# Sorted token rows widened from 130 to 144 words, and new rank numbers for the planner

## The reference, cut to what matters

```
x = x + 0.5 * ffn0(ln(x))      # gated low-rank mixture: softmax gate, 8 experts of rank 16
x = x + mamba(ln(x))           # in-projection, width-4 convolution, scan over 2048 steps, out-projection
x = x + 0.5 * ffn0(ln(x))
x = x + 0.5 * moe(ln(x))       # 8 experts, top 2 of each token, and a shared expert
x = x + attn(ln(x))            # linear attention, 16 heads of 8
x = x + 0.5 * moe(ln(x))
```

## Time and profile before

| | us |
|---|---|
| median of 3 runs | 842.06 (841.09 to 842.87) |
| the profiled execution | 838.86, of which the span is 837.5 |
| TensorE busy | 766.9 (92% of the span) |
| of it fillers (L558) | 70.6 |
| VectorE, ScalarE, GpSimd busy | 573.4, 559.3, 516.7 |
| mean granted TensorE clock | 0.975 |

### The profile page before, as it was taken

How to read it: one execution, slowest core, us unless ns; L and a number is a source line. 1 busy time by engine, 2 the same in 40 slices (tenths; PEclk the granted TensorE clock), 3 DMA queues, 4 the chain that set the end, 5 groups by cost and what they waited for, 6 DMA issues and landing times.

```text
span 837.5 us, 15645 instructions
## 1 busy us (share of the span) xinstructions
PE 766.9 (92%) x4762; PEld 604.3 (72%) x4762; DVE 573.4 (68%) x1960; ACT 559.3 (67%) x1305; POOL 516.7 (62%) x650
## 2 busy tenths in 40 slices
PE   7999999998898999988999999999999999997992
PEld 6668668785877776677877758867587876695771
DVE  5387579988899868767648884767975668633112
ACT  4888788796779688676677754685446577533551
POOL 4137527737837763898854487747775565774652
PEclk9998999998999999999999999999999999998997
DMA  9930000001100120212123212311422111217215
GB/s 326 406 140 2 1 1 1 2 2 39 52 1 8 36 61 23 62 42 75 43 71 92 56 52 71 119 30 49 127 65 59 44 49 33 68 57 221 83 58 169
DMA packets 43890, 60.70 MB, mean 72 GB/s; under 512 B 7083, under 2 KB 32939, under 8 KB 43595
## 3 DMA queue, kind: packets, MB, share of 16 engines
q1 hardware_dynamic: 33987, 39.36, 14.9%
q0 software_dynamic: 9536, 19.68, 7.0%
q10 hardware_dynamic: 288, 0.67, 0.2%
HBM read 26.61 MB, written 33.07 MB: 71 GB/s over the span
## 4 chain that ended last, share of the span: by engine, by line
PE 29%; POOL 22%; DVE 19%; issue 14%; DMA 8%; ACT 7%; SPq 0%; POOLq 0%; DVEq 0%; ACTq 0%
POOL sorted_x L1805 10%; PE psum L563 6%; PE psum L834 5%; PE psum L854 5%; POOL sent_y L1815 4%; DMA sent_y<-e_y,e_sx 3%; DVE m_cv L1066 2%; DMA e_sx<-sorted_x 2%; POOL m_ch L1743 1%; PE psum L558 1%; PE psum L643 1%; POOL m_ch L1746 1%; PE psum L876 1%; PE psum L735 1%; DMA c_ys<-sent_y 1%
## 5 line engine op out<-in xcount | busy, mean ns | idle before, releaser
L1815 POOL DMA_INDIRECT sent_y<-e_y,e_sx x170 | 166.9, 982 | 101.0 <-ACT e_y L1643 60.6
L1805 POOL DMA_INDIRECT sorted_x<-g_xn,r_slot x128 | 128.9, 1007 | 38.3 <-issue 28.3
L834 PE MATMUL psum<-gu_w,e_sx 128*128 x340 | 114.4, 466 | 0.7 <-issue 0.3
L1338 DVE TENSOR_TENSOR e_h<-e_h,psum 128x352 f32<-128x352 f32 x88 | 43.5, 505 | 95.8 <-ACT e_h L1635 95.7
L854 PE MATMUL psum<-d_w,e_h 88*128 x680 | 90.6, 280 | 2.6 <-DVE m_ch L1090 1.7
L854 PEld LDWEIGHTS psum<-d_w,e_h 88*128 88x128 f32 x680 | 84.2, 194 | 11.8 <-issue 9.5
L1643 ACT ACTIVATE e_y<-psum,e_sx 128x128 f32<-128x128 f32 x170 | 52.5, 363 | 49.0 <-PE psum L854 46.4
L834 PEld LDWEIGHTS psum<-gu_w,e_sx 128*128 128x128 f32 x340 | 60.1, 192 | 28.7 <-issue 7.1
L558 PE MATMUL psum<-ones 128*128 128x128 f32 x468 | 70.6, 293 | 3.7 <-POOL ones L1839 2.7
L1461 ACT ACTIVATE e_h<-psum 88x512 f32<-88x512 f32 x88 | 49.3, 574 | 36.3 <-PE psum L563 36.1
L558 PEld LDWEIGHTS psum<-ones 128*128 128x128 f32 x468 | 64.0, 207 | 7.2 <-issue 3.0
(11 more groups left out here) (265 smaller groups left out, 1933.9 us busy)
## 6 DMA issues: line engine op xcount, KB each, us to landing
e_sx<-sorted_x SPq DMA_DIRECT2D x82, 130.0 KB, 2.2
sorted_x<-c_ys SPq DMA_DIRECT2D x8, 975.0 KB, 19.7
c_ys<-sent_y SPq DMA_DIRECT2D x14, 512.0 KB, 4.8
sent_y<-e_y,e_sx POOLq DMA_INDIRECT x170, 2.3
sorted_x<-c_ys SPq DMA_DIRECT2D x4, 520.0 KB, 15.9
xs<-in_x SPq DMA_DIRECT2D x8, 256.0 KB, 7.2
sorted_x<-g_xn,r_slot POOLq DMA_INDIRECT x128
out<-xs SPq DMA_DIRECT2D x7, 256.0 KB, 3.7
```

Source lines behind the costliest of these rows:

```text
L834: last = e.matmul(two.banks[j].tile[:, 0:2 * IEXP], e_xT[k % SXS][:, j, :], gu_w[:, bass.ds(which[j] * (2 * IEXP), 2 * IEXP)], start=True, ...
L1805: e.indirect_dma_start(out=sorted_x[CHAIN_OF[g]], out_offset=bass.IndirectOffsetOnAxis(ap=r_slot[n][:, k, t:t + 1], axis=0), in_=rows[:, j ...
L1815: e.indirect_dma_start(out=sent_y[CHAIN_OF[g]], out_offset=bass.IndirectOffsetOnAxis(ap=e_sx[k % SXS][:, j, DM:DM + 1].bitcast(U32), axis= ...
```

## The change

The row of `sorted_x`, `g_xn` and `e_sx` grows from 130 to 144 words (576 bytes, a multiple of 64). EMPTY_ROWS goes from 15 to 14, so that `unused` still fits its tile (2016 words in place of 1950); the number of clearing DMAs stays 14. The 14 new words of each row in `g_xn` are set to zero once, by six memsets on GpSimd at the start. All rank tables have new numbers. The code of the stages is the same; lines from L1846 on move down by two.

```diff
-SENT = DM + 2
-EMPTY_ROWS = 15
+SENT = DM + 16
+EMPTY_ROWS = 14
...
-GATED = [-1497.43, -960.07, 235.63, 1059.97, -7983.26, -1651.28, -41121.12, -217474.65, -604379.49, -849493.79, 2025218.58, 2025219.86, 8147161894221.35, 6245036494796.88, 9945646075954.11, 4444332380753.18]
-SORTED = [-2090.99, 301.91, -1657.3, -35988.35, -539663.99, 494449.79, 1200.61, -2160876050918.97]
-SCATTERS = [-2102.77, -374.8, -3399.65, -875901.89, -1060663.42, -857995.38, 5024367203900.46, 6425558899159.76]
-PAIRED = [3666.91, -3680.96, -321147.12, -1076870.97, 1382196855041.05, 1516605603609.4, -19347204475812.39, -9460026041.51]
-PACE = [-1050.91, 43.59, 25911.68, 66896.07, 3527377721.29, 766276379171.74, 29710191757825.85, 70005041151.74]
-SENDS = [3831.16, -3506.7, -134882.98, -1595699.93, -816918.01, -3539908697451.05, 1830812465821.03, 40706064242.79]
+GATED = [-1612.12, -1346.31, 356.81, 1334.2, -2048.0, -1910.79, -101456.5, -269539.84, -35665391501.77, -410616469058586.44, 442199635419.06, 502734914612.92, 1552142795094442.8, -43274453972354.49, 1981894470395523.5, -1118408670439937.5]
+SORTED = [-2246.32, 1258.21, -3334.22, -36096.98, 1448911033546.08, 505016298414.97, -38562742267150.11, -598217000560311.0]
+SCATTERS = [344.97, -1816.91, -3712.68, -35939813952.68, -208340876042141.6, 29237801575472.65, 2778915344593449.5, 3026567072914857.0]
+PAIRED = [3695.57, -3222.66, -365441.24, -36419792749.16, -13224196291645.03, 4210780943512.94, -454154928134527.56, -1647290385447738.5]
+PACE = [-1122.96, 10.56, 23989.31, 68581921.67, 162723903713.99, 139491480699914.4, 1174660669112806.5, 6393651726682.28]
+SENDS = [3649.32, -3839.35, -55107.17, -36203751788.7, 32539564149069.16, 1265605042228444.5, 2774040927401660.5, 40704983681.34]
...
-KV = [-3161.35, -3477.72, -218282.65, -36067.44, 2173065613425.52, -902319.35, 2271812405962.31, 3814568062581.78]
+KV = [-3032.32, -3409.14, -276152.59, -80207.69, -36066720278.38, 1451984751506.02, -410688839305970.75, 143702267412699.53]
...
             e.memset(r_before[:, 1, 0:E1], 0.0).then_inc(*S.up("const"))
+            for n in range(KEPT):
+                e.memset(g_xn[n][:, :, DM + 2:SENT], 0.0)
```

More of the change, by code:

```diff
@@ L98 @@
 ATANH = [2.0 / (2 * k + 1) for k in range(8)]
[L102 to L105, removed]
+FIRST = [-2922.08, -2401.94, -1709.16, -1700.91, -1583.08, -1612.43, 376.46, 417.78]
@@ L106 @@
+AGAIN = [-960.85, -1032.71, -2157.16, -2516.16, 476.01, -2241.58, -3016.99, -3080.49]
+MAMBA = [-1739.62, -1693.62, -1056.95, -1066.84, -2194.24, 381.12, 3735.88, -5322.46]
+CHUNK_AT = [-1087.79, -1852.23, -1069.29, -1161.19, -1772.88, -855.06, -1041.13, -1030.56, -1025.62, -776.8, -1586.73, -455.61, -903.83, -1622.58, -1583.54, -1591.63, 367.78, 296.26, 347.39, -2403.13, 260.12, 414.62, 440.87, 370.95, -7605.45, -7662.02, -4057.85, -3749.59, -3745.39, -3740.45, -3713.07, -3404.84]
 TAP_STEP = -2.4
@@ L107 @@
 FOLD_AT = 35.0
-FINISH = [-1555.21, -913.54, -856.1, -2166.89, 1061.16, -3355.47, -3891.89, -3376.38]
-GATED = [-1497.43, -960.07, 235.63, 1059.97, -7983.26, -1651.28, -41121.12, -217474.65, -604379.49, -849493.79, 2025218.58, 2025219.86, 8147161894221.35, 6245036494796.88, 9945646075954.11, 4444332380753.18]
-SORTED = [-2090.99, 301.91, -1657.3, -35988.35, -539663.99, 494449.79, 1200.61, -2160876050918.97]
-SCATTERS = [-2102.77, -374.8, -3399.65, -875901.89, -1060663.42, -857995.38, 5024367203900.46, 6425558899159.76]
@@ L112 @@
-PAIRED = [3666.91, -3680.96, -321147.12, -1076870.97, 1382196855041.05, 1516605603609.4, -19347204475812.39, -9460026041.51]
-PACE = [-1050.91, 43.59, 25911.68, 66896.07, 3527377721.29, 766276379171.74, 29710191757825.85, 70005041151.74]
-SENDS = [3831.16, -3506.7, -134882.98, -1595699.93, -816918.01, -3539908697451.05, 1830812465821.03, 40706064242.79]
-COMBINED = [-18183.9, -8653.47, -118270.4, -110341.07, -742382.23, -875916.28, -7887759.42, 1363754074812.36, 53502778098.95, 72346421462.71, -62120096746.5, 72348063240.02, 2685.72, -5174.61, -5547.01, -7103.58]
@@ L116 @@
-KV = [-3161.35, -3477.72, -218282.65, -36067.44, 2173065613425.52, -902319.35, 2271812405962.31, 3814568062581.78]
-SECOND = [97099.17, -809153.13, -876124.06, -851076.21, 2269152799943.75, 5347987499104.99, 6232314056787.54, 1209.55]
+FINISH = [-838.34, -1060.83, -1443.51, -2242.63, 498.38, 116.18, -3212.05, -3164.46]
+GATED = [-1612.12, -1346.31, 356.81, 1334.2, -2048.0, -1910.79, -101456.5, -269539.84, -35665391501.77, -410616469058586.44, 442199635419.06, 502734914612.92, 1552142795094442.8, -43274453972354.49, 1981894470395523.5, -1118408670439937.5]
@@ new lines @@
+SENDS = [3649.32, -3839.35, -55107.17, -36203751788.7, 32539564149069.16, 1265605042228444.5, 2774040927401660.5, 40704983681.34]
+COMBINED = [-8015.11, -3000.99, -282100.63, -212517.46, -35987210115.56, -36066216093.46, -1734739926934.01, -35693160466.22, -1642308097568646.5, -39024453699689.71, -58311172712784.99, -45569380261851.71, 2869.03, -5207.28, -5390.58, -8109.89]
+KV = [-3032.32, -3409.14, -276152.59, -80207.69, -36066720278.38, 1451984751506.02, -410688839305970.75, 143702267412699.53]
@@ L119 @@
+SECOND = [160301.56, -35658142141.42, -35939813984.41, -35665391606.49, 823725072857151.9, 1259494977240303.2, 1106136945967049.9, 1209.55]
 TAPPED_BY = [sum(len(TAPPED[k // BLK_PER_BATCH]) for k in range(b)) for b in range(NBLK + 1)]
```

## The result

The changed kernel takes 845.18 us (median of 16 runs, 840.56 to 851.18) against 842.02 us (16 runs, 837.16 to 843.91): a ratio of 1.0049, 95% interval 1.003 to 1.0067. It is slower by half a percent, 4.1 us by the ratio. The profiled execution is one of the slower of its 16: 849.99 us, span 848.7, where the median's span would be 843.8.

A forecast was written before the change was run, and what follows sets the result against it. No single engine was taken as the bound, but the order of work, with slack thickest at the end. 838.86 us, four terms of 0 and -5 for the ranks gave 833.9; +3.2 made the median 837.1, range 823 to 853.

The forecast's parts named there:

- the slower side: Whole kernel: chance 0.31 for slower, beside 0.49 for faster and 0.20 for the same.
- Wider rows, loads, clearing, memsets: Scatters, expert loads, clearing and six start memsets: each priced at 0 us; loads could range from -2.3 to +0.5.
- The 2% that I allowed alignment: Scatters on the DMA engines: alignment worth at most 2% of 0.2 us on each engine per scatter, counted as nothing.
- the trace agrees with the rule: DMA price: 47.7 us/MB for 520-byte scatter rows against 46.6 for 512-byte sends, read as supporting the rule of 256-byte cuts.
- The new ranks: -5 us: Order on all engines: new rank tables save 5 us, between ends of -20 and +17.
- the tail's 20.4: TensorE in 725:775: 20.4 us without useful work, a quarter of which the new order was to recover.
- the four entries: GATED[13], GATED[15], KV[6], SORTED[6] now rank before every group 5 pair, so last gates and scatters should come sooner.
- My upper end, +17: GpSimd: worse order costs at worst one more stall like the 8.44 us at each of two places.
- the less than 30 that I had named as a sign: Tail: fillers and idleness of TensorE's last 100 us come to less than 30 us, from 34.3.
- GpSimd's wait: GpSimd after the burst of sends ending at 764.05: its idle wait of 8.44 us was to be gone.
- Sends fall behind: Rival: put-off group 5 sends delay the last scatters and `e_y` stops TensorE, +7 us, 849; chance 0.32.
- the point on which the prediction called itself wrong in advance: Wrong if the last scatter starts after 750 with TensorE's work behind it no shorter, or the gain lies before 600.

The follow-up runs named there:

- rows_only_5: Wider rows (144 words, clearing, memsets) with the old rank tables, against the kernel before at 842.16 us: 840.10 us, ratio 0.9980.
- gates_first: Kernel before with only GATED[13], GATED[15], KV[6] and SORTED[6] at their new values: 897.51 us against 889.79, ratio 1.0090.
- the halves: Kernel before with new ranks only up to expert round 1 (ratios 1.0233, 1.0385), or only for attention and round 2 (1.0676, 1.0767).
- first_new: Kernel before with only the table FIRST new (8 numbers): 983.10 us against 889.79, ratio 1.1067.
- after_same: The changed kernel itself measured again, against the kernel before at 841.01 us: 844.30 us, ratio 1.0042.
- before_fill08: Kernel before, old ranks, with fewer fillers (302 in place of 468): 841.67 us against 841.01, ratio 1.0017.
- rows_only: Wider rows with the old rank tables, against the kernel before at 903.8 us: 904.08 us, ratio 0.9994.
- rows_only_4: Wider rows with the old rank tables, in another job, against the kernel before at 889.79 us: 889.82 us, ratio 0.9989.

## Why the prediction was wrong

*The median and the sign.* Forecast 837.1 us, measured 845.18; inside the range of 823 to 853, but on the slower side, to which I gave 0.31.

*Wider rows, loads, clearing, memsets: taken at 0.* Right, by four runs with a mean ratio of 0.9998, of which one is at 842 us. Scatters cost GpSimd 959 ns as before, loads land in 2.3 us against 2.2, the memsets and the longer clearing held nobody up (the last clearing DMA starts at 30.7 in rows_only_5 in place of 29.8, and the first scatter starts at 188.4, before 189.4). The 2% that I allowed alignment was 4% by the byte for the scatters and 10% for the sends, and in time nothing that the ratio resolves, as the sum had it.

The Trainium skill's rule, cuts at 256 bytes ("DMA: Bandwidth & Descriptors", section "How a descriptor splits into AXI transactions"), gave 20.5 beats for the old rows and 21 for the new, so no gain by the row and, per byte, 20.5 / 520 against 21 / 576, 7.5% less; measured is 4.2% less by the byte, so in direction as the rule has it. But my "the trace agrees with the rule" for 47.7 against 46.6 us/MB was a poor reading. By the same estimate 512-byte rows that start at multiples of 256 take 16 beats, 21% less by the byte than the old rows; measured was 2.3% less. For the sends, whose length is the same in all kernels, the rule could act only through a start address, which no view shows.

*The new ranks: -5 us.* This is the step that failed: "Between ends that far apart I take a quarter of the tail's 20.4: -5 us." Behind it stood the step from raised ranks to earlier last scatters. Measured is +4.1 us by the ratio (ranks alone 1.0046), with the last scatter at 762.2, 754.1, 751.4 and 763.6 in the four profiles of the new ranks at 842 us, never before the 749.8 of the kernel before. Three things are wrong in it.

First, the reading of the diff. I named the four entries that move ahead of the pairs of group 5 and left out GATED[12] and GATED[14], which move back. Group 6 needs the gates i = 12 and 13, group 7 those of 14 and 15. Counted in pairs of group 5, GATED[12] goes from t = 8.7 to 11.1 and GATED[14] from 11.0 to 14.2, so by the ranks the later gate of each group didn't come forward. SORTED[6] stood below those pairs already. And in the 890 us condition gates_first has the last scatter 15.7 us later with the four entries alone. Why is argued, not shown: a rank decides only between pieces that are both ready, and a piece pushed ahead pushes something back on which a later one waits.

Second, the way: I read an effect out of single numbers of tables that have none by themselves where they were tried, as the halves and first_new show.

Third, where to look. I priced the tail and the slack. The profiles with the new ranks fall 8 to 15 us behind by the eighth scan block, before 430 us, and win back 2 to 8 of it later. And I took the useful time of TensorE as fixed, while it lies between 695 and 713 us in the table above and goes with the clock. My upper end, +17, was written as stalls on GpSimd; that isn't what the profiles show.

*The tail.* The slack of the last 100 us of TensorE work is 31.2 us (737:837: 11.7 idle, 19.6 fillers) after 34.3, 3 us less, but not the less than 30 that I had named as a sign. Behind TensorE's end lie 17.2 us after 18.1, and from the last scatter to the end 86.5 after 87.7. GpSimd's wait is 9.62 us, not gone.

*The rivals.* "Sends fall behind" gave the right sign with the wrong mechanism: the new order was already 15.0 us behind at 428 us, before any of these sends. Two sends fewer than before stood behind the last scatter, worth 2.5 us by their pitch. The result also meets the point on which the prediction called itself wrong in advance: the last scatter is later than 750, and from it to TensorE's end it is 69.3 us after 69.6.

**What stays open.** That the loss belongs to the ranks is shown; through what is not. The runs give two readings of the clock's share that don't agree. Over the 29 executions of the kernel before in the job of after_same, 0.01 less of mean clock goes with 5.8 us more (correlation -0.80), by which the 0.0045 that after_same has less would be 2.6 of its 3.3 us. But before_fill08, in the same job at the same mean clock as after_same (0.9676 and 0.9672), is 2.6 us faster than it, 841.67 against 844.30, so the rest may be waits of the order itself. before_fill08 also has 166 fillers less to run, so it doesn't change the clock alone. Ranks and clock were never changed apart. And why the same ranks gain where the kernel before takes 890 us isn't settled.

## What to carry to other kernels

When the ranks that set an order change, don't read the effect from single ranks: list every entry that moves, also those that move the other way. Count TensorE's useful time and its slack apart, beside the clock, and take more than one profile of a kernel: here two profiles of one kernel differed by 7 us. Split a change into its parts on one chip before explaining any of them; here the part that looked like the point (the wider, aligned rows) was nothing that could be told in time. Compare only with the old kernel of the same job, and look whether the sign holds in a second job.

## What the runs showed of the hardware

**The same kernel at 841 and at 890 us.** The chip alone doesn't decide it: one chip gave the kernel before 841.01 us in one job and 889.79 in a later one, another 903.8 and then 842.16. The profiles of the long jobs show waits that the others don't have. The view of waits of rows_only (span 906.0):

```profile
ACT e_h L1461 <- remote: 54.9, 6, 18.9
DVE xs L1209 <- remote: 42.9, 5, 14.5
```

and the longest of them in the timeline, of TensorE, VectorE and ScalarE:

```profile
790.47 2.84 PE L783 MATMUL psum<-w_gates,s_sg 118*128 118x128 f32 x24
793.15 0.82 PE L563 MATMUL psum<-w_ffn,e_h 128*88 128x128 f32 x6
...
805.37 1.12 DVE L1209 SCALAR_TENSOR_TENSOR xs<-psum,g_s,xs 128x128 f32<-128x128 f32 x4 [14.45 <-remote]
...
808.23 0.86 ACT L1461 ACTIVATE e_h<-psum 88x512 f32<-88x512 f32 x2 [17.39 <-remote]
```

VectorE's L1209 waits for the matmuls of L783, whose records end at 793.3, and starts at 805.4; the records of matmul ends are modelled, so TensorE may really have been held up. "remote" is the profile's word for a releaser that it doesn't have. In this stretch GpSimd issues 16 scatters back to back; up to 255 us, where there are scatters too but no expert matmuls beside them, this profile and the others keep pace (last scatter of the first group issued at 212.1 there and 212.9 before). In the chain of rows_only waits for an unknown releaser make up 7.9% of the span, 72 us, and the difference to the profile of the kernel before is 68.5 us. That the two are so near is luck: in rows_only_4 it is 4.0% of 893.9, 36 us, for a difference of 56. What holds TensorE up was not tried.

**Row width and the price of another transfer.** 512-byte rows from an SBUF tile that didn't change cost 47.6, 42.2 and 47.0 us of engine time per MB when other tiles had rows of 130, 144 and 146 words. The scatters of those rows themselves cost 47.5, 45.5 and 48.1. In the time of the kernel neither could be told (ratio 0.9980, interval 0.9960 to 1.0000).
